# Two blocks of experts ahead of the first tile's keys, and a later request for the third set of weights

## The reference

```python
proj = u @ W_in                      # z, x, Bg, Cg, dd_dt, dd_A, trap, angles
adt = minimum(-softplus(dd_A), -A_FLOOR) * dt;  dt = softplus(dd_dt + dt_bias)
theta = cumsum(angles * dt)          # over the tokens, per head
K = rope(rmsnorm(Bg) * B_w + B_bias, theta);  Q = rope(rmsnorm(Cg) * C_w + C_bias, theta)
S = (Q @ K^T) * weights * decay      # inside a chunk, lower triangle
y = S @ x + Q @ state;  state = decay_of_chunk * state + K^T @ (weights * x)
attn = ((y + D * x) * silu(z)) @ W_out
# experts: the top 2 of 16 per token, weights renormalised
h = silu(xn @ W1[e]) * (xn @ W3[e]);  out += w * (layernorm(h @ W2[e]) * gamma[e] + beta[e])
result = u + attn + out
```

## Time and profile before

| | |
|---|---|
| median of 3 runs | 284.83 us |
| the profiled execution's own time | 285.08 us |
| its span, first to last instruction | 283.4 us |
| mean granted TensorE clock | 0.963 of full |
| busy in the span: PE, DVE, POOL, ACT | 89%, 78%, 74%, 53% |
| DMA over the span | 61.55 MB, 217 GB/s |

### The profile page before, as it was taken

One profiled execution on the slowest core, in us unless ns is written; L12 is line 12 of the kernel. 1 busy time (PEld: TensorE's weight loads), 2 busy tenths in 40 slices (PEclk: granted clock), 3 DMA queues, 4 the chain that ended last, 5 costly groups with the idle time before them and its releaser, 6 DMA issues.

```text
span 283.4 us, 7397 instructions
## 1 busy us (share of the span) xinstructions
PE 251.7 (89%) x2155; PEld 219.3 (77%) x2158; DVE 221.5 (78%) x607; ACT 149.7 (53%) x508; POOL 208.7 (74%) x291
## 2 busy tenths in 40 slices
PE   2999995799999999999999999999999999999600
PEld 0858863688997998899889979997998899889400
DVE  4778998958787969796978778787969796977436
ACT  1765989455456453755363645456453755362033
POOL 8658997858887787888887878787787876665400
PEclk9999999699999999999999999999999999999955
DMA  5630917966978778988888899879878887770095
GB/s 156 220 94 13 325 57 225 319 176 196 260 225 273 247 226 248 264 243 243 237 278 253 222 251 264 243 216 249 288 229 256 262 240 248 238 220 21 23 270 172
DMA packets 68855, 61.55 MB, mean 217 GB/s; under 512 B 6608, under 2 KB 52304, under 8 KB 68816
## 3 DMA queue, kind: packets, MB, share of 16 engines
q1 hardware_dynamic: 66256, 55.83, 65.5%
q0 software_dynamic: 2560, 5.25, 6.7%
HBM read 56.27 MB, written 4.78 MB: 215 GB/s over the span
## 4 chain that ended last, share of the span: by engine, by line
PE 56%; DVE 21%; issue 7%; ACT 5%; DMA 4%; POOL 4%; SPq 1%; DVEq 1%; POOLq 0%; ACTq 0%
PE bank L868 15%; PE bank L911 6%; PE bank L811 5%; PE bank L803 4%; PE bank L863 4%; PE bank L795 4%; PE bank L761 3%; DVE rot L1330 2%; PE bank L766 2%; PE bank L845 2%; DMA decay<-res_dram 2%; DVE sd L1346 2%; PE bank L907 2%; DMA blk<-xn_dram,gidx 2%; DVE rot L1329 1%
## 5 line engine op out<-in xcount | busy, mean ns | idle before, releaser
L868 PE MATMUL bank<-blkT,w_up 128*128 128x128 f32 x512 | 64.7, 281 | 0.4 <-issue 0.4
L868 PEld LDWEIGHTS bank<-blkT,w_up 128*128 128x128 f32 x512 | 62.0, 196 | 2.5 <-issue 2.1
L631 POOL DMA_INDIRECT res_dram<-xrow,sidx x40 | 40.7, 1018 | 22.3 <-DVE xrow L1408 18.0
L577 POOL DMA_INDIRECT blk<-xn_dram,gidx x40 | 42.1, 1053 | 8.6 <-issue 7.4
L911 PE MATMUL bank<-w,xrow 128*128 128x128 f32 x256 | 34.6, 278 | 0.3 <-DVE xrow L1395 0.3
L1086 ACT ACTIVATE xrow<-bank 128x512 f32<-128x512 f32 x40 | 25.2, 629 | 15.7 <-PE bank L868 11.1
L911 PEld LDWEIGHTS bank<-w,xrow 128*128 128x128 f32 x256 | 31.1, 192 | 1.6 <-issue 1.6
L1380 DVE TENSOR_TENSOR xrow<-xrow,bank 128x512 f32<-128x512 f32 x40 | 27.3, 683 | 4.6 <-issue 4.0
L1312 DVE SCALAR_TENSOR_TENSOR kq<-sd,rms,bias_kq 128x512 f32<-128x512 f32 x32 | 23.3, 767 | 8.6 <-POOL rms L588 8.0
L624 POOL TENSOR_TENSOR rstd<-mv,mhalf 128x1 f32<-128x1 f32 x40 | 25.1, 628 | 1.5 <-DVE mv L1392 1.3
L1080 ACT ACTIVATE blkT<-bank 128x128 f32<-128x128 f32 x40 | 12.2, 305 | 21.2 <-PE bank L854 21.2
(11 more groups left out here) (246 smaller groups left out, 625.3 us busy)
## 6 DMA issues: line engine op xcount, KB each, us to landing
w_up<-in_L_ffn_W_dram SPq DMA_DIRECT2D x96, 256.0 KB
w<-in_L_ffn_W_dram SPq DMA_DIRECT2D x48, 256.0 KB
e_row<-e_dram SPq DMA_DIRECT2D x16, 256.0 KB
decay<-l_dram SPq DMA_DIRECT2D x4, 512.0 KB, 5.7
gam<-in_L_ffn_gamma_dram SPq DMA_DIRECT2D x32, 64.0 KB
shift_y<-in_L_ffn_beta_dram SPq DMA_DIRECT2D x32, 64.0 KB
acc<-in_L_attn_u_dram SPq DMA_DIRECT2D x4, 256.0 KB, 3.7
xn_dram<-xrow SPq DMA_DIRECT2D x4, 256.0 KB, 5.1
```

The costliest lines, as they stand in the source:

```text
L577: g.indirect_dma_start(out=blk[:, b % SLOTS, :], out_offset=None, in_=xn_dram, in_offset=bass.IndirectOffsetOnAxis(ap=gidx[:, entry(b):ent ...
L631: g.indirect_dma_start(out=res_dram, in_=res[:, b % HALF, :], in_offset=None, out_offset=bass.IndirectOffsetOnAxis(ap=sidx[:, entry(b):ent ...
L868: last = m(bank[out][:, c * P:(c + 1) * P], w_up[:, u % SETS, n, c * P:(c + 1) * P], blkT[:, b % 2, :], start=True, stop=True)
```

## The change

Six things change. SP waits for block 0's gathered tokens before it requests the sets of block 2. The sums of angles of batch 2 go to bank 2 instead of bank 7. PE gets six 512-column products of constants before block 0, and the list of iteration 0 becomes blocks 0 and 1 as far as `down(0)`; keys, queries and the state product of tile 0 go to iteration 1, behind `rise(2)`. ACT copies block 0 ahead of the sines, and the two copies of x stand in a function of their own behind block 2's copy. DVE takes `product(0)` ahead of `rot_cosine(0)`, and `product(1)`, `diagonal(0)` and `diagonal(1)` ahead of `norm_y(0)`. In iteration 1 DVE takes `product(2)` ahead of `norm_kq(1)`.

```diff
+    WARM_BLOCKS = 6
-    THETA = (4, 5, 7, 3)
-    ARMS_READ = (7, 8, 6, 0)
+    THETA = (4, 5, 2, 3)
+    ARMS_READ = (7, 8, 0, 0)
...
@@ SyncE, the loop over blocks
+                    if b == 2:
+                        sp_.wait_ge(blk_in[0], 16)
                     for u in sets(b):
                         load(u)
...
@@ TensorE
+                if THETA[b] == 2:
+                    pe.wait_ge(lrow_ready, 1)
...
             def turn_kq(t):
                 pe.wait_ge(s["k_rot"], 2 * (t + 1))
                 if t == 0:
-                    pe.wait_ge(lrow_ready, 1)
-                    pe.wait_ge(theta_ready, CUT.index(3) + 1)
+                    pe.wait_ge(theta_ready, NBATCH)
...
@@ down(b)
-                if b == 0:
-                    pe.wait_ge(theta_ready, NBATCH)
...
+            def first_blocks():
+
+                pe.wait_ge(sidx_ready, 1)
+                for _ in range(WARM_BLOCKS):
+                    m(bank[6][:, :], ones_h[:, :], neg_h[:, :, :].rearrange("p h i -> p (h i)"), start=True, stop=True)
+                turn_block(0)
+                pe.wait_ge(theta_ready, 2)
+                rise(0)
+                turn_block(1)
+                rise(1)
+                turn_block(2)
+                down(0)
...
+                if first:
                     project_x(t)
...
-                if first and not begins:
+                if first and t > 1:
                     project_bc(t)
-                if b0 is not None and not begins:
+                if b0 is not None:
                     rise(b0)
                     turn_h(b0 - 1)
+                if t == 1:
+
+                    turn_kq(0)
+                    turn_block(b0 + 1)
+                    down(b0 - 1)
+                    state_product(0)
+                    project_bc(t)
+                    turn_block(b0 + 2)
                 if second:
                     scores(t - 1)
-                if b0 is not None and not ends_ and not begins:
+                if b0 is not None and not ends_ and t > 1:
                     down(b0 - 1)
                     turn_block(b0 + 2)
...
@@ ScalarE
+            def first_blocks():
+
+                nc.scalar.preload_act_table_set("silu_and_others")
+                act.wait_ge(rest_in, 16 * RESTS)
+                out_block(0)
+                sines(0)
+                silu(0)
+                out_block(1)
+                weigh(0)
+                silu(1)
+                out_block(2)
+                move_x(0)
+                gates(0)
...
-                    weigh(t)
-                    gates(t)
-                    out_block(b0)
+                if t == 1:
                     silu(b0)
-                    out_block(b1)
-                    out_kq(t)
-                elif first:
+                    out_kq(0)
+                    out_block(b0 + 1)
+                if first:
                     squares(t)
                     weigh(t)
                     gates(t)
+                    move_x(t)
...
@@ VectorE
+            def first_blocks():
+
+                mean_square(0)
+                cut_turns(0)
+                dve.wait_ge(rest_in, 16 * RESTS)
+
+                dve.wait_ge(theta_psum, NBATCH)
+                weigh_bc(0)
+                cut_turns(1)
+                norm_kq(0)
+                product(0)
+                rot_cosine(0)
+                cut_turns(3)
+                rotate(0)
+                cut_turns(2)
+                product(1)
+                diagonal(0)
+                diagonal(1)
...
+                if first:
                     mean_square(t)
                     weigh_bc(t)
-                    norm_kq(t)
+                    if t > 1:
+                        norm_kq(t)
                 if b0 is not None:
                     if first:
                         shift_block(b0 - 2)
                     product(b0)
+                if t == 1:
+                    norm_kq(t)
```

More of the change, by code:

```diff
@@ L913, in down @@
                 last.then_inc(f["y_psum"], 1)
+            def first_blocks():
[9 more added lines that the diff above has]
+                down(0)
             def iteration(t, first, second, blocks):
                 b0, b1, b2 = blocks
[L917 to L925, removed]
-                elif first:
+                ends_ = t == NT
+                if t == 0:
+                    first_blocks()
+                    return
+                if first:
                     project_x(t)
@@ L1067, in gates, with move_x @@
                 a(tile, tile, ACT.Silu).then_inc(s["gate_ready"], 1)
+            def move_x(t):
                 again(act, s["inter_psum"], t - 1)
@@ L1092, in out_h @@
                     a(hT[:, :], bank[6][:, :], ACT.Copy).then_inc(f["turned"], 1)
+            def first_blocks():
[10 more added lines that the diff above has]
+                gates(0)
             def iteration(t, first, second, blocks):
                 b0, b1, b2 = blocks
[L1096 to L1099, removed]
+                if t == 0:
+                    first_blocks()
+                    return
                 if first:
                     sines(t)
-                if begins:
-                    weigh(t)
-                    gates(t)
-                    out_block(b0)
+                if t == 1:
                     silu(b0)
-                    out_block(b1)
-                    out_kq(t)
-                elif first:
+                    out_kq(0)
+                    out_block(b0 + 1)
+                if first:
                     squares(t)
@@ L1112, in iteration @@
                     gates(t)
+                    move_x(t)
                 for b in (b0, b1):
                     if b is not None:
-                        if not (begins and b is b0):
+                        if t > 1 or b == b1:
                             out_block(b + 1)
@@ L1447, in iteration @@
                     norm_y(b1 - 2)
-                if begins:
-                    diagonal(0)
-                elif first:
+                if first:
                     rot_cosine(t)
-                if first and not begins:
+                if first:
                     rotate(t)
```

## The result

| | before | after |
|---|---|---|
| median of 4 runs (lowest to highest) | 284.54 us (284.24 to 285.39) | 289.01 us (288.75 to 289.66) |
| ratio, 95% interval | | 1.0145 (1.0118 to 1.0171) |
| the profiled execution's own time | 285.08 | 289.66 |
| its span | 283.4 | 287.9 |
| mean granted TensorE clock | 0.963 | 0.963 |

The change makes the kernel slower by 1.45%, some 4.1 us by the ratio; the medians differ by 4.5. In lines of `after` all numbers are some 5 to 35 higher than before: L859 is a block's transpose, L873 `rise`, L914 `down`, L808 the state product, L772 `project_bc`, L1413 `product`.

The account below looks back on a forecast made before the run. PE is busy in nearly every slice after the second stage's start, so a shift there, set by block 0's gather and DVE's list, reaches the end: +2.1 - 0.5 (gather) + 1.3 (clock) = +2.9 us, 287.7; range 283.6 to 289.2.

Parts of the forecast that it names:

- T itself: Start of turn_block(0) on PE: 51.20 before, expected 0.5 us earlier after the change.
- g: Gather of block 0: lands earlier because SP holds set 2 back; between nothing and 2.3 us, taken as 0.5.
- the wait holds back nothing: Rival at block 0's gather: it lands when it did, set 3 last; +3.4 to +4.3 us, chance 0.09.
- `product(0)`: DVE's first product: starts once both products are in PSUM, T + 2.90 at full clock, plus the low clock's cost.
- c: What a low PE clock adds to product(0), through rise(0): 0 to 1.75 us, taken as 1.3.
- DVE's list to POOL's square: DVE from product(0) through rot_cosine, cuts, rotate, a product and diagonal(0): 0.61, 1.29 and 4.67 us.
- The square, `diagonal(1)`, `norm_y(0)`: POOL's square_own(1) takes 0.64 us plus 0.1 for the signal, then DVE's diagonal and norm take 1.56.
- `down(1)` to `project_bc(1)`, to `mean_square(1)`, to the end of `gate_y(0)`: PE's state product and projection take 0.89 + 0.84 us, then 1.29 to mean_square(1), then 7.7 on DVE.
- Who holds `down(1)`: PE waits at down(1) a microsecond or more for norm_y(0), as it writes the bank that norm_y(0) reads.
- the rival of the longer low clock: Rival: rise(1) and down(0) on PE also run slowly, so down(1) comes later; +3.7 to +4.4 us, chance 0.12.
- The faster rival: Rival: PE does not wait for DVE's list in down(1); mark moves -0.8 to -2.6 us, 283.1, chance 0.14.

Follow-up runs that it names:

- e8_bridge_pad: Changed kernel with 22 warm products instead of 6 and 16 one-column copies on ACT ahead of its first block copy; 287.99 us, 1.0143 against the kernel before.
- e4_rotate_first: Changed kernel with DVE's rotation of tile 0 ahead of product(0) and ACT's sines ahead of block 0's copy; 288.29 us, 1.0109 against the kernel before.
- e7_all: Changed kernel with 22 warm products, ACT's 16 copies, no SP wait, rotation first, project_bc(1) ahead of rise(2); 285.30 us, 1.0010 against the kernel before.
- e3_bc_early: Changed kernel with project_bc(1) ahead of rise(2), ACT's squares ahead of silu(2), POOL's finish(0) and rms_pow(1) ahead of weigh_q(0); 286.70 us.
- e9_bridge_diagonal: Kernel before with 21 products of constants ahead of block 0's turn and diagonal(1) between weigh_bc(1) and norm_kq(1); 283.70 us, 0.9964 against the kernel before.
- e2_bridge: Changed kernel with 22 warm products on PE instead of 6; 289.63 us, 1.0152 against the kernel before.
- e11_before_product2: Kernel before with shift_block(0) and product(2) ahead of norm_kq(1), nothing else of the change; 286.25 us, 1.0073 against the kernel before.
- e5_before_bridge: Kernel before with 21 products of constants on PE ahead of block 0's turn; 284.52 us, 0.9999 against the kernel before.

## Why the prediction was right, and where its sizes were off

The direction held, and so did the mechanism in the main: DVE's list begins late, and the projection behind `down(1)` waits for its end. Times are from T, the start of `turn_block(0)`:

- *T itself*: forecast 0.5 earlier, measured 0.68 later. The term g (the gather gains from the wait) failed: the means with and without the wait differ by 0.15, so the rival "the wait holds back nothing" was right on this point. 0.26 of the 0.68 is a first stage that ended later, the rest the gather's scatter.
- *`product(0)`*: T + 4.0 forecast (with c = 1.3), T + 4.74 measured. The clock had fallen before `rise(0)`, so it cost the whole 1.75, the upper end given, and the transpose and the copy around the fall took 0.3 more. The trace of `e8_bridge_pad` puts the clock at 2.0.
- *DVE's list to POOL's square*: 6.57 forecast, 5.95 measured. `rot_cosine` took 0.67 from the start of its pair to the next instruction (57.22 to 57.89), not 1.29: beside gathers alone on POOL it ran at 0.42 for each half. The prediction says that it took the uncontended rows; this row it took from a place where POOL's `square_own` and `finish` ran beside DVE.
- *The square, `diagonal(1)`, `norm_y(0)`*: 0.74 and 1.56 forecast, 0.74 and 1.57 measured. *`down(1)` to `project_bc(1)`, to `mean_square(1)`, to the end of `gate_y(0)`*: 1.73, 1.29, 7.7 forecast; 1.80, 1.35, 7.82 measured. DVE's idle time ahead of `mean_square(1)`, with ACT's squares as the releaser, was to be some 3 us and was 3.30.
- *Who holds `down(1)`*: I expected PE to stand idle there for a microsecond or more, with `norm_y(0)` as the releaser. No idle time shows. PE came at 65.03 by its own list, 0.15 after `norm_y(0)` ended at 64.88: the two lists tied. I had PE's list at `project_bc(1)` by T + 11.0, so at `down(1)` by some T + 9.3, and took the wait for x as covered; with `rise(0)` and `rise(1)` slow and that wait it came at T + 13.15. So at that clock a shorter list on DVE alone would gain nothing, by the estimate given with `e4_rotate_first`. At full clock (`e8_bridge_pad`) `down(1)` began at T + 11.15, 0.15 after `norm_y(0)`, near the T + 11.8 of the forecast.
- *The rest*: over the chain +3.86 against +3.4 forecast, and T +0.68 against -0.5. The 0.5 in iteration 2 stood nowhere in the forecast: I had taken the shift at `gate_y(0)` as final, and `product(2)` ahead of the norm as a pure filler; that the norm behind it holds POOL's share of the rotation had no term.

So the +2.9 of the forecast became +5.1 by: the gather, 0.9 (0.5 not gained, 0.42 later in this execution); the first stage, 0.26; the clock, 0.45; a turn and copy at the lower level, 0.3; DVE's rotation, -0.6; the last four steps, 0.4; POOL in iteration 2, 0.5. The third stage took 0.65 off again, which no term foresaw. The profiled execution itself, at 289.66, lies above the range and the median 0.2 inside it, so that the range held is in part luck. Nearest to what was measured is the rival of the longer low clock, +3.7 to +4.4: `rise(1)` did run slowly in part (2.76), as it says, though `down(0)` did not.

The faster rival needed `norm_y(0)` to be over by T + 9.5. In `e4_rotate_first` it was over at T + 10.6, against T + 13.0 in after, and PE's list, with the place of `project_bc(1)` on it, held as well. `e7_all` mends DVE's order, the clock, SP's wait and that place together and comes back to the old time, where nothing is won; whether all of them are needed for it was not tried (`e3_bc_early` alone came to 286.70). `e9_bridge_diagonal` shows what was to be had instead: keep the old order, bridge the gather, and take one DVE sum out of POOL's way.

Open: why the gather takes 4.9 to 6.0 us from issue to PE's turn, from one execution to the next; why the clock stayed low for 3.4 us in one trace and 6.8 in another of the same order on PE; whether ACT's stop is an instruction fetch; and whether moving the state product in `e7_all` ahead of `down(1)` would gain, which was not tried.

## What to carry to other kernels

Work brought forward gains only if what it displaces was not the filler of a wait: here DVE's rotation had run while the gather did, and behind `product(0)` it left DVE idle for 5.68 us. Follow a late instruction to every engine that waits for it, and one iteration further: `product(2)` ahead of the norm cost 0.5 us in iteration 2, in all eight kernels that had it. Look at the granted clock of both traces before a difference between them is put down to an edit (`e4_rotate_first`). And before pricing a moved operation by its old row, see what POOL did beside that row.

## What the runs showed of the hardware, unexpected

- ACT stood still for 2.63 us ahead of a copy for which it waited 0.41 in another trace, in a stretch with one packet in the queue of kind "instruction"; with 16 more small instructions ahead of it the stop was not there (`e2_bridge`, `e8_bridge_pad`, one trace each).
- A DVE sum of two SBUF tiles that ran beside a POOL product of 1.28 us ended 0.55 us after it, whether it began 0.7 us after POOL or, by the profile's starts, 0.66 before it: 1.17, 2.17 and 2.49 us for the same work that takes 0.69 alone (`before`, `e11_before_product2`, `e5_before_bridge`).
- Holding back SP's later requests left that queue with 0.01 to 0.05 MB in the microsecond before block 0's turn, against 0.30 to 0.36, and the gather came no earlier (mean 5.37 us from issue to turn against 5.52, five traces each).
- A bridge of 21 or 22 products kept the clock up for `rise(0)` (2.02 instead of 3.75), but PE stood idle from 57.4 to 60.2, and the granted clock fell at 61.1, after the work had begun again, and was back at 64.5 (`e2_bridge`, `rise(2)` 3.46 instead of 1.95).
